# Relative-position attention moved onto row and column groups of the array, with its position products inside the same loop

## The reference

```
x  = layernorm(src)*g1 + b1
q, k, v = x @ wq, x @ wk, x @ wv              (16 heads of 16)
p  = position_encoding @ wp                    (199 relative distances)
ac = q . k          bd_full = q . p            (100 x 199 per head)
bd[i, j] = bd_full[i, i - j + S - 1]           (each row shifted by one)
att = softmax((ac + bd) / 4) @ v @ wo
src = src + att
x2 = layernorm(src)*g2 + b2                    (input of the experts)
```

## Time and profile before

| | us |
|---|---|
| median of 3 runs | 2831.58 (2828.62 to 2831.77) |
| profiled execution | 2840.09 |
| its span | 2838.3 |
| TensorE busy | 2356.7 (83%) |
| VectorE busy | 1539.9 (54%) |
| ScalarE busy | 1141.0 (40%) |
| the stage up to the end of its attention | 1012.48 to 1234.72 |

### The profile page before, as it was taken

One profiled execution on the slowest core, in us unless ns is written; L12 is line 12 of the kernel. 1 busy time (PEld: TensorE's weight loads), 2 busy tenths in 40 slices (PEclk: granted clock), 3 DMA queues, 4 the chain that ended last, 5 costly groups with the idle time before them and its releaser, 6 DMA issues. The chain is left out here.

```text
span 2838.3 us, 44441 instructions
## 1 busy us (share of the span) xinstructions
PE 2356.7 (83%) x15408; PEld 1882.4 (66%) x15408; DVE 1539.9 (54%) x3310; ACT 1141.0 (40%) x3119; POOL 516.4 (18%) x715
## 2 busy tenths in 40 slices
PE   5799574669999965969877787979996999699997
PEld 3566341237777755869766335869995566599997
DVE  2566648984444432755555553545654556455555
ACT  3556344543343422623210323533332366455553
POOL 0110017971000022300133111000003322100000
PEclk8699788899999987979888888979996899699998
DMA  2000012210000024224200003412210000133331
GB/s 101 9 1 2 31 61 73 70 45 30 1 1 1 1 67 124 56 85 152 81 25 16 1 0 95 129 61 95 90 51 25 11 8 4 62 106 105 106 109 53
DMA packets 57458, 152.20 MB, mean 54 GB/s; under 512 B 16913, under 2 KB 31861, under 8 KB 55234
## 3 DMA queue, kind: packets, MB, share of 16 engines
q1 hardware_dynamic: 57286, 149.99, 17.0%
HBM read 138.48 MB, written 11.50 MB: 53 GB/s over the span
## 5 line engine op out<-in xcount | busy, mean ns | idle before, releaser
L2262 PE MATMUL ps<-l1a_zc,tables_sb 128*128 128x400 f32 x256 | 106.9, 549 | 98.4 <-POOL l1a_zc L2191 61.8
L2262 PEld LDWEIGHTS ps<-l1a_zc,tables_sb 128*128 128x128 f32 x256 | 46.4, 199 | 159.0 <-POOL l1a_zc L2191 90.2
L1760 ACT ACTIVATE l1x_probs<-ps,l1x_nmax 100x361 f32<-100x361 f32 x128 | 70.7, 557 | 189.7 <-DVE l1x_nmax L1842 189.7
L2202 POOL TENSOR_TENSOR l1a_dbx<-l1a_dx,l1a_rows 128x400 f32<-128x400 f32 x128 | 130.2, 1053 | 7.1 <-DMA l1a_rows<-l1a_rows_spilled 5.0
L2610 DVE TENSOR_TENSOR l3f_act_out<-l3f_act_out,l3f_gates 128x800 f32<-128x800 f32 x80 | 79.4, 992 | 82.1 <-ACT l3f_act_out L2566 82.1
L2614 DVE TENSOR_TENSOR l3f_hg_low<-l3f_act_out,l3f_hg_high 128x800 fp32r<-128x800 f32 x80 | 79.5, 993 | 62.9 <-ACT l3f_hg_high L2572 62.9
L2454 PE MATMUL ps<-l3f_x_high,l3f_w_high 128*128 128x400 f32 x320 | 111.4, 348 | 0.0
L2453 PE MATMUL ps<-l3f_x_high,l3f_w_low 128*128 128x400 f32 x320 | 110.9, 347 | 0.5 <-DVE l3f_w_low L2544 0.5
L2566 ACT ACTIVATE l3f_act_out<-ps,l3f_biases 128x800 f32<-128x800 f32 x80 | 74.3, 929 | 92.0 <-PE ps L2455 92.0
L2455 PE MATMUL ps<-l3f_x_low,l3f_w_high 128*128 128x400 f32 x320 | 110.8, 346 | 0.0
L2454 PE MATMUL ps<-l3f_hg_high,l3f_w_high 128*128 128x400 f32 x320 | 110.2, 344 | 0.0
(11 more groups left out here) (666 smaller groups left out, 6686.7 us busy)
## 6 DMA issues: line engine op xcount, KB each, us to landing
l3f_landing<-l_ffn_units SPq DMA_DIRECT2D x40, 513.0 KB, 3.4
l3f_gates<-l3f_gates SPq DMA_DIRECT2D x40, 400.0 KB, 3.5
l2x_a_taps<-l2x_taps_spread SPq DMA_DIRECT2D x8, 1912.5 KB
l2f_landing<-l_ffn_units SPq DMA_DIRECT2D x17, 771.0 KB, 4.3
l1a_rows<-l1a_rows_spilled SPq DMA_DIRECT2D x32, 400.0 KB, 3.5
l1f_gates<-l1f_gates SPq DMA_DIRECT2D x16, 800.0 KB, 4.0
l1f_positions<-l1f_bd SPq DMA_DIRECT2D x16, 621.9 KB
l1f_landing<-l_ffn_units SPq DMA_DIRECT2D x16, 512.0 KB, 3.5
```

Of the source, the lines that this page charges most:

```text
L2202: pool.tensor_tensor(dbx[:, n % BUFS, :], dx[:, j, m, :], rows[:, g % RING, 0, :], ALU.mult).then_inc(s.dbx_ready, 1)
L2262: pe.matmul(y_bank(m), st.ident, zc[:, n % DONE, :], start=(i == 0), stop=(i == NS - 1)).then_inc(s.sum_done, 1)
```

## The change

`l1_ffn` no longer projects q in its first block, drops the two turns of position products and the call of `attention`, and calls `self_heads` with three new arguments: its own input `xT`, the inner normalisation `inner`, and `between`, which holds `pT` and the two access patterns of the DRAM scratch. In it:

- The position products use the q copies and row groups of the scores. A part is a quarter batch: four products (two heads of different parity in two row groups) of 199 columns into two banks; VectorE copies one bank and ScalarE the other into `staged` (three buffers, half a batch each). The first 12 parts (three batches) run ahead of everything and use all eight banks; the parts of batch j+3 are spread over iteration j and share banks 0 and 1 with the scores.
- SyncE stores each half batch as rows of 8 x 199 numbers without gaps, and loads the shifted term into `bd`.
- VectorE's maxima take the term of their head in the place of the mask.
- In every call without convolution, `scores(j+1)` is issued in iteration j, ahead of `turn(4j+1)`, instead of at the head of iteration j+1. This holds for the first stage too.
- `self_heads` has nine more semaphores, in each of its three calls.

```diff
+            def load(sp, j):
+                for unit in (2 * j, 2 * j + 1):
+                    sp.wait_ge(bd_stored[unit % STAGED], 16 * (unit // STAGED + 1))
+                if j >= 2:
+                    sp.wait_ge(s.masked_ready, G * (j - 1))
+                sp.dma_start(bd[:, j % 2], between.skewed(j)).then_inc(bd_loaded[j % 2], 16)
...
+                    for j in range(B):
+                        if j >= AHEAD:
+                            load(sp, j - 1)
+                        for unit in (2 * j, 2 * j + 1):
+                            sp.wait_ge(s.bd_first_copied, 2 * unit + 2)
+                            sp.wait_ge(s.bd_second_copied, 2 * unit + 2)
+                            sp.dma_start(between.rows(j)[...], staged[:, unit % STAGED]).then_inc(bd_stored[unit % STAGED], 16)
+                        if j < 2:
+                            load(sp, j)
...
                     rstd_pool(pool, norm, s, j)
+                    if inner:
+                        pool.tensor_tensor(x_b(j), norm.resid[:, j, :], x_b(j), ALU.add).then_inc(s.x_summed, 1)
...
+                def positions(part):
...
+                    if part >= 4 * AHEAD:
+                        pe.wait_ge(s.masked_ready, G * (j - AHEAD) + 2)
+                        pe.wait_ge(s.bd_first_copied, part)
+                        pe.wait_ge(s.bd_second_copied, part)
+                    elif part >= 4:
+                        pe.wait_ge(s.bd_first_copied, part - 3)
+                        pe.wait_ge(s.bd_second_copied, part - 3)
+                    for par in range(2):
+                        for i in range(2):
+                            r = 2 * (q % 2) + i
+                            group = slice(SLOT * r, SLOT * (r + 1))
+                            last = pe.matmul(st.ps[0:S, bd_bank(part) + i, par * REL:(par + 1) * REL], q_pad[group, par, m, j, :], between.pT[group, m, :],
+                                             start=True, stop=True, tile_position=(SLOT * r, 0))
...
                 def scores(j):
+                    if between:
+                        pe.wait_ge(s.bd_first_copied, min(4 * (j + AHEAD), 4 * B))
+                        pe.wait_ge(s.bd_second_copied, min(4 * (j + AHEAD), 4 * B))
```

More of the change, by code:

```diff
@@ L36 @@
 InnerNorm = namedtuple("InnerNorm", "gain shift turned")
+Between = namedtuple("Between", "pT rows skewed")
 Convolution = namedtuple("Convolution", "windows keep mask")
@@ L1131, in _, with self_heads @@
                         copy_out(x)
-def self_heads(nc, st, name, w, bias=None, mask=None, conv=None):
+def self_heads(nc, st, name, w, bias=None, mask=None, conv=None, xT=None, inner=None, between=None):
     H, HD = 16, 16
@@ L1322, in _ @@
                     project("q", 0, part)
+                if between:
+                    pe.wait_ge(s.k_copied, KT)
+                    for part in range(4 * AHEAD):
+                        positions(part)
+                    pe.wait_ge(s.bd_first_copied, 4 * AHEAD)
+                    pe.wait_ge(s.bd_second_copied, 4 * AHEAD)
                 project("v", 0, 0)
                 for j in range(B + 2):
-                    if j < B:
+                    if j == 0 or conv and j < B:
                         scores(j)
@@ L1341, in _ @@
                         values(j - 1)
+                    more = between and j + AHEAD < B
+                    if more:
+                        positions(4 * (j + AHEAD))
+                    if 1 <= j <= B:
                         on_the_side("inv", j - 1)
+                    if more:
+                        positions(4 * (j + AHEAD) + 1)
                     if j < B:
@@ L1346, in _ @@
                         turn(G * j)
+                    if more:
+                        positions(4 * (j + AHEAD) + 2)
                     if j + 1 < B:
@@ L1350, in _ @@
                         on_the_side("k", 1, j)
+                    if more:
+                        positions(4 * (j + AHEAD) + 3)
+                    if not conv and j + 1 < B:
+                        scores(j + 1)
                     if j < B:
@@ L1398, in _ @@
                 copy_q(0)
+                if between:
+                    for part in range(4 * AHEAD):
+                        copy_positions(part)
                 for j in range(B + 2):
@@ L1412, in _ @@
                         copy_out("inv", j - 1)
+                    more = between and j + AHEAD < B
+                    if more:
+                        copy_positions(4 * (j + AHEAD))
                     if j == 0:
@@ L1507, in _ @@
                         add_output(j - 2)
+                    more = between and j + AHEAD < B
+                    if more:
+                        copy_positions(4 * (j + AHEAD))
                     if j < B:
                         maxima(G * j + (1 if conv else 2))
+                    if more:
+                        copy_positions(4 * (j + AHEAD) + 1)
+                    if j < B:
                         if conv:
```

204 lines of the change are left out of this document (95 added, 109 removed).

## The result

The changed kernel takes 2796.1 us (median of 4 runs, 2794.32 to 2804.73); the kernel before took 2831.68 beside it (4 runs). The ratio is 0.9886 [0.9869, 0.9904]; the medians differ by 35.6 us. The profiled execution is the slowest of the four, 2804.73 us with a span of 2803.0, so the spans differ by 35.3.

The account below looks back on a forecast made before the run. Old position turns were taken as store-bound, attention as TensorE-bound. First exponential 1067 + 18.5 + 68 + 20.6 + 23.6, plus 3.7 + 0.3, gives 1201.7 against 1238.44; with first stage -4 and semaphores +1.3, -39.4: 2792 us, range 2774 to 2810.

Parts of the forecast that it names:

- What is removed: Changed stage: separate q projection and barrier 11.6 us, position turns to first exponential 90.7 us, attention itself 103.7 us.
- The prologue: 12 position parts ahead of the loop: stores set the pace, first exponential at 1067 us, bounds 1062 and 1070.
- Five batches that carry positions: Loop batches 0 to 4: handovers through banks 0 and 1 set the period; 18.5 us, then four of 17.
- Semaphores: Barriers, 0.07 us per semaphore: nine more add 0.65 us in each of two other stages, 0.3 in the changed one.
- warm loop: Rival for the loop with positions: TensorE's 68% holds the clock up, batches 14.5 us; -53, 2779 us; chance 0.17.
- cold loop: Rival for the loop with positions: handover gaps keep 1.2 GHz, batches 20.4 us; -22, 2809 us; chance 0.10.
- Batches 5 and 6: Last loop periods, without position parts: 10.3 us each, 20.6 us together.
- the drain: End of the changed stage's attention: 21.9 us as in the first stage, plus added VectorE operations and a wait, 23.6.
- The move of the scores: Scores of batch j+1 issued in iteration j: 0.4 to 0.8 us less per batch, 4 us in the first stage.
- Row groups do not overlap: Rival for position products of 199 columns: parts cost 1.5 us, loop 15 us more; -24, 2807 us; chance 0.05.
- slower by DMA: Rival for the loop: loads and stores at three times today's cost, 38 us per batch; +66, 2897 us; chance 0.03.
- A drain of the array: Changes between full-array and row-group work in the loop: priced at nothing, at most 0.1 us each, 5 us in all.

Follow-up runs that it names:

- Experiment 7: The changed kernel with four staging buffers instead of three; 2784.8 us, 0.9851 to the kernel before.
- experiment 9: The changed kernel with four staging buffers and two surplus full-array products per batch; 2778.78 us, 0.9801 to the kernel before.
- Experiment 10: The changed kernel with four staging buffers and the second half's q and k projections moved into the prologue; 2781.37 us, 0.9810 to the kernel before.
- experiment 11: The changed kernel with four staging buffers, second-half projections in the prologue and two surplus full-array products per batch; 2784.53 us, 0.9822 to the kernel before.
- experiment 8: The changed kernel with two surplus full-array products per batch on the side bank; 2789.27 us, 0.9869 to the kernel before.
- experiment 6: The changed kernel with part 3 of each loop batch in two banks of its own; 2795.04 us (one run).
- experiment 1: The kernel before with only the scores moved into the previous iteration in calls without convolution; 2823.55 us against 2826.24, 0.9982.
- experiment 2: The changed kernel with the scores back at the head of their iteration in all calls; 2800.47 us, 0.9908 to the kernel before.
- experiment 12: The changed kernel with four buffers, projections in the prologue, surplus products and positions four batches ahead; 2779.91 us, 0.9826 to the kernel before.

## Why the prediction was right, step by step, and where a size was off

The order of events, the waits and the overlaps came as forecast. That the total did so within 4 us is in part luck. The attention part gained 28.5 us instead of 36.7. The first stage gained 7.5 instead of 3.4 (4 less 0.65 for semaphores), mostly with its clock, and the stage behind the changed one 3.2 for a reason that is open; the rest differs by 3 us the other way.

**What is removed** was exact, since it was read between marks of the timeline.

**The prologue** was right in mechanism and within 2 us: positions start 26.3 us into the stage (forecast 27.4), the first exponential comes at 52.5 (54.5). Experiment 7 shows the queue as its cause: with one more buffer, nothing waits for the store that stands behind load 0, and 7.5 us go; experiments 9, 10 and 11 show it again (44.3 to 44.7). The estimate that two stores take 9 us from the first issue came out (1033.34 to 1042.28), and load 0 landed 6.2 us after its issue. Two prices in the prologue were off and hidden. A part costs 0.49 us at full clock when parts follow each other, against 0.75; consecutive parts use the other two row groups (how much of the gain comes from that was not measured). Alone in the loop a part costs 0.92 (L1328 at 1061.56; forecast 0.75) and at the low clock 1.65 (1.4).

**"Five batches that carry positions", 18.5 + 4 x 17 = 86.5 us**, is the term that was mis-sized: it measured 94.99, 8.5 more. The chain itself held. Its marks can be read in the batch of experiment 8 at a clock of 0.98, which starts at 1093.21:

```profile
1096.35 0.92 PE L1331 MATMUL ps<-l1f_pT,l1f_q_pad 32*100 32x199 f32 x8
...
1099.66 0.92 PE L1331 MATMUL ps<-l1f_pT,l1f_q_pad 32*100 32x199 f32 x8 [0.91 <-ACT l1f_staged L1472]
...
1104.23 0.92 PE L1331 MATMUL ps<-l1f_pT,l1f_q_pad 32*100 32x199 f32 x8 [0.79 <-issue]
1105.81 0.96 PE L1351 MATMUL ps<-l1f_kT,l1f_q_pad 32*100 32x100 f32 x32 [0.67 <-DVE l1f_staged L1544]
```

Part 0 ends 4.1 us into the batch (forecast 3.8), part 1 at 7.4 (6.9), part 3 at 11.9 (11.4), the scores at 13.6 (13.1), and the period is 14.70 (14.5), with the two surplus products in it. At 1.2 GHz the forecast was 20.4: experiment 6 has 20.10 at 0.50, and 21.55 was measured in experiment 11 with the surplus products. Laying a line between the two forecasts in 1/clock gives 17.0 at 0.70, where 17.23 and 17.27 were measured, and 18.6 at 0.59, where 18.60 was (with surplus products the batches lie up to 1 us above it: 16.98 at 0.80). So two things remain:
- *The projections of the second half.* Batches 0 and 1 took 20.40 and 21.49 us where 18.5 and 17 were forecast: 6.4 of the 8.5. Forecast was 1.5 us for the q projection, in batch 0 alone; it took 4.83. The k projections in batches 0 and 1 (3.04 and 3.01 us) were forgotten. By the line batch 0 should take 17.4 (0.67) and batch 1 18.8 (0.58), 5.7 less than measured. That is an estimate and rather too low, since the first two batches have no output work yet, which the line contains. Experiment 10 took the projections away and the two batches lost 7.3 us at a lower clock. The trace of before had it: in its first stage the first periods were 14.6 and 12.1 us, the last 10.3 (first exponentials at 32.78, 47.36 and 59.47, and the earlier trace rows). I read the mean of a window over all batches and not the batches one by one.
- *The clock.* 17 us stand for 0.70. Batches 2 to 4 took 2.1 us more than forecast, and 1.6 of them are batch 2 at 0.59. Batch 1 had 0.58, for which the line gives 1.8 more. How the 6.4 of the first two batches divide between clock and projections is not shown. Neither "warm loop" nor "cold loop" came true. The warm rival put the 0.99 of the old attention down to TensorE being busy 91% of it; that reason is not borne out, since experiment 11 has a batch at 0.50 with TensorE busy 90%.

The Trainium skill (TensorE: Matmul & The Clock Gate, HAM oscillation) states that repeated waits in a loop re-throttle the array. The trace agrees in part: the loop had 0.64 on average, not a steady 0.50, and experiment 11 came to 0.50 with TensorE busier, not idler.

**Batches 5 and 6** took 11.67 and 10.25 (10.3 each; 11.67 at a clock of 0.56), **the drain** 24.3 (23.6), the barrier 3.76 (3.7 + 0.3). **Semaphores** were priced right in the other two stages: from the last copy to the next stage's weights it is 4.13 us instead of 3.49 in the first and 3.77 instead of 3.13 in the eighth, 0.64 for nine (forecast 0.65). The attention part as a whole went from 226.0 to 197.4, -28.5 against -36.7; the 8.5 of the loop make up that difference; the other terms nearly cancel (-2.0, +1.3, +0.7, -0.2).

**The move of the scores** was forecast at 0.4 to 0.8 per batch, 4 us; experiments 1 and 2 give 0.37 to 0.48, 3 us. The seven periods of the first stage gained 7.7, and the further 4.7 go with a clock of 0.83 instead of 0.72; experiment 2 has a higher clock with the old order as well. In the loop with positions, where it was to shorten the batches too, it cost 0.5 us in each batch that can be compared (experiment 2). The price per batch was worked out for a loop in which turns stand ahead of the scores; here the last part's copies end just ahead of them, so there is little for the move to take off, and it puts a turn and two copies behind them.

**Row groups do not overlap** and **slower by DMA** did not happen: parts of 0.49 us where 1.5 was that rival's price, and VectorE never waits for a load in the loop. **A drain of the array** shows no gap either: part 0 follows the values at once.

```profile
1102.37 0.89 PE L1384 MATMUL ps<-l1f_probsT,l1f_vals 100*32 100x100 f32 x32 [0.64 <-issue]
1103.20 0.92 PE L1328 MATMUL ps<-l1f_pT,l1f_q_pad 32*100 32x199 f32 x8
...
1108.14 0.91 PE L1372 MATMUL ps<-tables_sb,l1f_probs 100*100 100x100 f32 x4
1108.97 1.65 PE L1328 MATMUL ps<-l1f_pT,l1f_q_pad 32*100 32x199 f32 x8
1110.55 2.03 PE L1288 MATMUL ps<-weights,l1f_xT 128*100 128x256 f32 x4
```

The Trainium skill (TensorEngine Tiling (Array Packing), Key Properties) says that a change of tiling mode drains the engine. In these rows full-array and row-group work follow each other with no idle time shown, so the trace does not bear out a visible price. Ends of products are modelled in it, though, and a part between full-array work takes 0.92 us where one in a row of parts takes 0.49; whether a drain has a share in these 0.43 us no run shows, nor the 0.1 us that the prediction allows as a bound.

**Sum.** -28.5 (attention) + 0.5 (experts) - 7.5 (first stage) - 3.2 (the stage behind) + 3.4 elsewhere = -35.3. The -3.2 in the attention stage behind the changed one is open. Its operations are the same, it took 127.88 in experiment 1 (with the old code ahead of it) and 124.6 in all kernels with the new; most of it falls in its second half. No experiment looked for the cause.

## What to carry to other kernels

In a loop of handovers between engines add up the chain at both clocks and interpolate in 1/clock. Then list, batch by batch, what stands only in the first ones: the projections stood in two batches of eight, and these two made 6.4 of the 8.5 us of error, while a window over all of them hid them. On a queue that issues in order, ask what is ready behind a transfer that waits: one more staging buffer took 7.5 us off the prologue. The whole kernels differ by some 10 us (ratios 0.9886 and 0.9851 to the kernel before), and their intervals just touch.

When an experiment shortens a piece, compare batches at the same clock before judging it: short products seemed to be worth 1 us per batch and were worth 3.2 at 1.2 GHz, and two equal sums hid a batch at 1.2 GHz. And a reordering that helps where one wait ends last can cost where another does, as the move of the scores did in the loop with positions.

## What the runs showed of the hardware

- The clock does not follow TensorE's busy share alone. With full-array products it was 0.99 at 91% busy; with row-group products in the loop 0.59 at 85% (15.89 of 18.60 us), and 0.50 at 90% (19.32 of 21.55 us) in experiment 11. The same products take longer at a low clock (1.65 us against 0.92), so a busy share read there is itself higher by it and can't forecast the clock.
- Two surplus full-array products per batch went with single batches at 0.93 to 0.98 (experiments 8, 9, 11 and 12), and without them none from batch 1 on was above 0.70 with parts of full size. They do not bring it about reliably: in experiment 11, with the projections no longer in the batches, the first three were at 0.50 (the surplus products stand from batch 1 on).
- Between kernels with the same code in a stage its time moves by 6 us with the clock: the first stage took 102.1 us in experiment 8 (its seven periods 64.4 us at 0.95) and 108.4 in the changed kernel (70.5 at 0.83).
- Eight records of 32 rows and 199 columns took 0.92 us alone at 2.4 GHz, 1.65 at 1.2 GHz, and 0.49 at 2.4 GHz in a row of such groups. With 20 columns they still took 0.53 and 0.86: about half of a part's price does not go with its columns.
- A semaphore cost 0.07 us at the barrier (nine more: 3.49 to 4.13 and 3.13 to 3.77 us).
- A store of 0.64 MB whose data were ready at 1035.2 was issued at 1042.66, behind a load that waited for earlier stores, and its buffer came free 8.5 us after that.
